# Row halves, a third score bank and a longer lead in a 32-head cross attention

## The reference, cut to what matters

```
n  = layernorm(x)                                  # 4 x 256 x 256
q  = n.reshape(4, 256, 32, 8)                      # 32 heads of 8
k = v = ctx.reshape(4, 256, 8, 8)                  # 8 groups, 4 heads share one
p  = softmax(q @ k.T / sqrt(8))                    # 256 x 256 for each head and batch
x  = x + (p @ v).reshape(4, 256, 256)
```

## Time and profile before

| | |
|---|---|
| median of 3 runs | 805.69 us (805.66 to 806.32) |
| the profiled execution's own time | 806.62 us |
| its span in the trace | 804.8 us |
| PE, DVE, ACT, POOL busy over the span | 89%, 72%, 53%, 25% |
| feed-forward stage | ends at 467 us |
| cross attention | 572.3 to 705.5 us of the span |
| its first and last value product | 599.42 and 702.61 us |

### The profile page before, as it was taken

How to read it: one execution, slowest core, us unless ns; L and a number is a source line. 1 busy time by engine, 2 the same in 40 slices (tenths; PEclk the granted TensorE clock), 3 DMA queues, 4 the chain that set the end, 5 groups by cost and what they waited for, 6 DMA issues and landing times. The chain is left out here.

```text
span 804.8 us, 13314 instructions
## 1 busy us (share of the span) xinstructions
PE 716.4 (89%) x4826; PEld 464.7 (58%) x4826; DVE 577.6 (72%) x1117; ACT 425.7 (53%) x888; POOL 198.6 (25%) x298
## 2 busy tenths in 40 slices
PE   5999989999999999999746569999489999879997
PEld 3555666666676766666422435566344444468886
DVE  5578678686767768677489855575669999665665
ACT  4558754544636454462659555555356666533322
POOL 2423010303113030321317124220121111362450
PEclk9999999999999999999979679999859999969999
DMA  4725432120211112010052016220110323303111
GB/s 121 188 67 159 152 73 69 51 56 25 79 26 56 30 51 75 6 44 14 15 162 49 9 28 176 68 55 2 32 31 22 88 64 88 113 2 107 60 46 53
DMA packets 50272, 52.50 MB, mean 65 GB/s; under 512 B 10116, under 2 KB 40900, under 8 KB 50100
## 3 DMA queue, kind: packets, MB, share of 16 engines
q1 hardware_dynamic: 49574, 51.32, 23.3%
q10 hardware_dynamic: 634, 0.33, 0.2%
HBM read 26.84 MB, written 2.04 MB: 36 GB/s over the span
## 5 line engine op out<-in xcount | busy, mean ns | idle before, releaser
L427 DVE TENSOR_REDUCE a_nm<-ps 128x2 f32<-128x512 f32 (+1 forms) x112 | 75.3, 688 | 28.1 <-PE ps L723 19.4
L2500 DVE TENSOR_REDUCE x_nm<-ps 128x2 f32<-128x512 f32 x128 | 84.9, 686 | 12.4 <-PE ps L2641 10.1
L2585 ACT ACTIVATE x_pt<-ps 128x1024 f32<-128x1024 f32 x64 | 62.5, 1021 | 34.6 <-PE ps L2669 33.9
L1537 PE MATMUL ps<-m_xp,m_mp 128*128 128x512 f32 x288 | 75.4, 398 | 1.0 <-DVE m_wr L1227 1.0
L1408 ACT ACTIVATE m_junk<-ps,m_nm 128x256 bf16<-128x256 f32 x128 | 58.7, 485 | 22.7 <-DVE m_nm L1244 22.7
L1191 POOL TENSOR_SCALAR fw<-fw,finv 128x256 f32<-128x256 f32 x24 | 11.7, 486 | 216.3 <-PE ps L1615 216.3
L2641 PE MATMUL ps<-kx,a_qs 96*128 96x256 bf16 x256 | 53.1, 296 | 8.1 <-DMA a_qs<-a_ks 6.4
L1537 PEld LDWEIGHTS ps<-m_xp,m_mp 128*128 128x128 f32 x288 | 50.8, 188 | 14.7 <-issue 5.3
L3069 PE MATMUL ps<-x_xp,x_wp 128*128 128x512 f32 x216 | 55.2, 406 | 0.0
L1207 DVE TENSOR_TENSOR m_qcs<-ps,mw_tab 64x512 f32<-64x512 f32 x64 | 44.0, 688 | 7.3 <-PE ps L1537 4.2
L1214 DVE TENSOR_TENSOR m_qcs<-ps,mw_tab 128x512 f32<-128x512 f32 x64 | 41.1, 684 | 7.5 <-PE ps L1537 7.2
(11 more groups left out here) (306 smaller groups left out, 1687.3 us busy)
## 6 DMA issues: line engine op xcount, KB each, us to landing
a_qs<-a_parts SPq DMA_DIRECT2D x48, 128.0 KB
a_ks<-a_parts SPq DMA_DIRECT2D x48, 128.0 KB
m_q<-m_qs SPq DMA_DIRECT2D x32, 128.0 KB
x_gb<-scr_g SPq DMA_DIRECT2D x8, 512.0 KB, 3.6
fw<-in_f_w SPq DMA_DIRECT2D x12, 256.0 KB
a_qs<-a_ks SPq DMA_DIRECT2D x48, 64.0 KB
mw_wq<-in_m_wq SPq DMA_DIRECT2D x8, 256.0 KB, 2.9
mw_wo<-in_m_wo SPq DMA_DIRECT2D x8, 256.0 KB, 2.7
```

The source lines that it names most:

```text
L427: dve.tensor_reduce(dst, src, AX.X, ALU.max, negate=True).then_inc(mx_done.sem, 1)
L1537: mm = pe.matmul(c.ps[:, QB_BANKS[k], :], mp[:, p % 2, w, dt, tile * P:(tile + 1) * P], xp[:, x, dt, half_cols(half)], start=((dt, w, x) = ...
L2500: dve.tensor_reduce(nm[:, n % ITEMS, QT * u:QT * u + QT], c.ps[:, u % 2, :].rearrange("p (t k) -> p t k", t=QT), AX.X, ALU.max, negate=Tru ...
L2585: act.activation(pt[:, n % 2, kt, :], c.ps[:, 2 + 2 * kt:4 + 2 * kt, :].rearrange("p b n -> p (b n)"), ACT.Exp, scale=SCALE).then_inc(exp_ ...
```

## The change

- Scores contract 48 rows and turned scores 50. Units of 4 items alternate between rows 0 to 49 and rows 64 to 113 of the query tile (`BASES`); the key tile holds its terms and ones twice, once for each half. No zeros are written. A slot holds two units, so a unit waits for the unit six before it.
- `LAG` is 5 and `TLAG` 4. In the loop the scores of item n + 5 and the turned scores of item n + 1 always lie in different row halves, and `side_by_side` issues them interleaved: one score matmul, one turned-score matmul, one score matmul, four times an item.
- From item 5 on scores take banks 0, 1 and 7 in turn. The turned maxima move from bank 7 to the unused half of bank 6 from item 4 on (`max_bank`).
- Both value products and then the transpose of maxima stand at the end of TensorE's loop.
- `outputs` moves from VectorE to ScalarE, at the end of ScalarE's loop. The two exponentials now stand next to each other, and `max_rows` after them.
- The warm-up has a fifth item of scores, after a `max_transpose(3)`.

```diff
-    GROUPS, S_ROWS, T_ROWS, HD = 8, 96, 98, 8
+    GROUPS, S_ROWS, T_ROWS, HD = 8, 48, 50, 8
+    BASES = (0, 64)
...
     def send(self, sp):
+        for base in self.BASES:
+            sp.dma_start(self.kx[base + self.S_ROWS:base + self.T_ROWS, :, :],
+                         self.ones[0:2, :].unsqueeze(1).broadcast_to([2, self.GROUPS, TOK])).then_inc(self.sent.sem, 16)
         for part, done in enumerate((self.hi_done, self.mid_done, self.lo_done)):
             sp.wait_ge(done.sem, 1)
             for term, p in enumerate((0, 1, 2, 0, 1, 0)):
                 if p == part:
-                    sp.dma_start(self.kx[term:TERMS * self.HD:TERMS, :, :], self.parts[:, part, :]).then_inc(self.sent.sem, 16)
-        sp.dma_start(self.kx[self.S_ROWS:self.T_ROWS, :, :],
-                     self.ones[0:2, :].unsqueeze(1).broadcast_to([2, self.GROUPS, TOK])).then_inc(self.sent.sem, 16)
-        sp.wait_ge(self.sent.sem, 16 * (TERMS + 2))
+                    for base in self.BASES:
+                        sp.dma_start(self.kx[base + term:base + self.S_ROWS:TERMS, :, :], self.parts[:, part, :])\
+                            .then_inc(self.sent.sem, 16)
...
-    LAG, TLAG = 4, 3
+    LAG, TLAG = 5, 4
...
+        def own_rows(n, first, last):
+            base = BASES[n // 4 % 2]
+            return slice(base + first, base + last)
+        def queries(n, first, last, h, count=1):
+            at = n % 4 * 4 + h
+            return qx[own_rows(n, first, last), n // 8 % RINGS, at:at + count, :]
+        def score_bank(n, u):
+            i = 4 * n + u
+            return i % 2 if n < LAG else (0, 1, 7)[(i - 4 * LAG) % 3]
+        def max_bank(n):
+            return c.ps[0:MAXR, 7, 0:SEQ] if n < TLAG else c.ps[0:MAXR, 6, SEQ:2 * SEQ]
...
                         if p == part:
-                            sp.dma_start(qx[term:TERMS * HD:TERMS, k % RINGS, :, :], parts[:, dt, part, seq_cols(b)])\
-                                .then_inc(part_in[k].sem, 16)
+                            sp.dma_start(qx[BASES[k % 2] + term:BASES[k % 2] + S_ROWS:TERMS, k // 2 % RINGS, :, :],
+                                         parts[:, dt, part, seq_cols(b)]).then_inc(part_in[k].sem, 16)
...
                     k, step = divmod(n + 6, 4)
                     if RINGS <= k < UNITS and step < 3:
-                        if step == 0:
-                            sp.wait_ge(st_done.sem, st_done.at(8 * (k - RINGS + 1)))
+                        if step == 0 and k >= 2 * RINGS:
+                            sp.wait_ge(st_done.sem, st_done.at(8 * (k - 2 * RINGS + 1)))
                         send(k, step, (hi_done, mid_done, lo_done)[step])
...
                     for u in range(4):
                         dve.wait_ge(s_done.sem, s_done.at(4 * n + u + 1))
                         dve.tensor_reduce(nm[:, n % ITEMS, QT * u:QT * u + QT],
-                                          c.ps[:, u % 2, :].rearrange("p (t k) -> p t k", t=QT),
+                                          c.ps[:, score_bank(n, u), :].rearrange("p (t k) -> p t k", t=QT),
                                           AX.X, ALU.max, negate=True).then_inc(mx_done.sem, 1)
-                def outputs(n):
-                    b, g = place(n)
-                    dve.wait_ge(av_done.sem, av_done.at(n + 1))
-                    if b >= 2 and g == 0:
-                        dve.wait_ge(dense_out.sem, dense_out.at(64 * (b - 1)))
-                    dve.tensor_scalar(av[:, b % 2, g, :], c.ps[:, 6, 0:SEQ], 1.0, None, ALU.mult)\
-                        .then_inc(out_done.sem, 1)
                 def quotients(s):
                     heads = WIDTH[s] // HD
...
                 maxima(2)
                 remainder(3)
                 maxima(3)
+                maxima(4)
                 for n in range(N - LAG):
                     maxima(n + LAG)
-                    outputs(n)
                 for n in range(N - LAG, N):
-                    for s in LAST_SLOTS[n]:
+                    for s in LAST_SLOTS.get(n, ()):
                         quotients(s)
-                    outputs(n)
                 for s in END_SLOTS:
                     quotients(s)
...
                 def max_rows(n):
                     act.wait_ge(tr_done.sem, tr_done.at(n + 1))
-                    act.activation(mT[:, n % ITEMS, :], c.ps[0:MAXR, 7, 0:SEQ], ACT.Copy).then_inc(mt_done.sem, 1)
+                    act.activation(mT[:, n % ITEMS, :], max_bank(n), ACT.Copy).then_inc(mt_done.sem, 1)
                     if n < TLAG:
                         act.wait_ge(mt_done.sem, mt_done.at(n + 1))
                         act.dma_start(shift_rows(n), mT[:, n % ITEMS, :]).then_inc(m_in[n % ITEMS].sem, 16)
+                def outputs(n):
+                    b, g = place(n)
+                    act.wait_ge(av_done.sem, av_done.at(n + 1))
+                    if b >= 2 and g == 0:
+                        act.wait_ge(dense_out.sem, dense_out.at(64 * (b - 1)))
+                    act.activation(av[:, b % 2, g, :], c.ps[:, 6, 0:SEQ], ACT.Copy).then_inc(out_done.sem, 1)
                 def exponentials(n, kt):
                     if n >= 2:
...
                 exponentials(0, 1)
                 max_rows(2)
                 middle(3)
+                max_rows(3)
                 for n in range(N - 1):
                     exponentials(n + 1, 0)
+                    exponentials(n + 1, 1)
                     if n + TLAG < N:
                         max_rows(n + TLAG)
-                    exponentials(n + 1, 1)
+                    outputs(n)
+                outputs(N - 1)
             @block.tensor
             def _(pe):
...
                                               c.ident[:, :])
                     mm.then_inc(xn_tr.sem, 1)
-                def scores(n, u):
-                    if n >= N:
-                        return
-                    b, g = place(n)
+                def may_score(n, u):
                     if u == 0 and n % 4 == 0:
                         pe.wait_ge(part_in[n // 4].sem, part_in[n // 4].at(16 * TERMS))
-                    if n > 0 or u > 1:
-                        pe.wait_ge(mx_done.sem, mx_done.at(4 * n + u - 1))
-                    for qt in range(QT):
-                        mm = pe.matmul(c.ps[:, u % 2, qt * SEQ:(qt + 1) * SEQ],
-                                       queries(slice(0, S_ROWS), n, u).squeeze(1)[:, qt * P:(qt + 1) * P],
-                                       kx[0:S_ROWS, g, seq_cols(b)], start=True, stop=True)
-                    mm.then_inc(s_done.sem, 1)
+                    i = 4 * n + u
+                    if i == 4 * LAG + 2:
+                        pe.wait_ge(mt_done.sem, mt_done.at(TLAG))
+                    elif i > 4 * LAG + 2:
+                        pe.wait_ge(mx_done.sem, mx_done.at(i - 2))
+                    elif i > 1:
+                        pe.wait_ge(mx_done.sem, mx_done.at(i - 1))
+                def score(n, u, qt):
+                    b, g = place(n)
+                    return pe.matmul(c.ps[:, score_bank(n, u), qt * SEQ:(qt + 1) * SEQ],
+                                     queries(n, 0, S_ROWS, u).squeeze(1)[:, qt * P:(qt + 1) * P],
+                                     kx[own_rows(n, 0, S_ROWS), g, seq_cols(b)], start=True, stop=True)
+                def scores(n, u):
+                    may_score(n, u)
+                    score(n, u, 0)
+                    score(n, u, 1).then_inc(s_done.sem, 1)
                 def max_transpose(n):
                     if n >= N:
...
                     pe.wait_ge(nl_done.sem, nl_done.at(n + 1))
                     both = nms[:, n % ITEMS, :, :].rearrange("p a n -> p (a n)").rearrange("p (r t) -> p t r", t=QT)
                     for qt in range(QT):
-                        mm = pe.matmul(c.ps[0:MAXR, 7, qt * P:(qt + 1) * P], both[:, qt, :], c.identb[:, :],
+                        mm = pe.matmul(max_bank(n)[:, qt * P:(qt + 1) * P], both[:, qt, :], c.identb[:, :],
                                        start=True, stop=True)
                     mm.then_inc(tr_done.sem, 1)
-                def scores_t(n, kt):
-                    if n >= N:
-                        return
-                    b, g = place(n)
+                def may_score_t(n, kt):
                     if kt == 0:
                         pe.wait_ge(m_in[n % ITEMS].sem, m_in[n % ITEMS].at(16 * (n // ITEMS + 1)))
                     if n:
                         pe.wait_ge(exp_done.sem, exp_done.at(2 * n - 1 + kt))
                     elif kt:
                         pe.wait_ge(rest_done.sem, rest_done.at(2))
-                    for h in range(0, 4, 2):
-                        mm = pe.matmul(c.ps[:, 2 + 2 * kt + h // 2, :],
-                                       kx[0:T_ROWS, g, b * SEQ + kt * P:b * SEQ + (kt + 1) * P],
-                                       queries(slice(0, T_ROWS), n, h, 2).rearrange("p h q -> p (h q)"),
-                                       start=True, stop=True)
```

(48 more changed lines are left out.)

10 lines of the change are left out of this document (4 added, 6 removed).

## The result

The changed kernel takes 794.52 us (median of 4 runs, 792.98 to 795.49). The kernel before, measured beside it, takes 806.01 (805.66 to 808.08). The ratio is 0.9855, with a 95% interval of 0.984 to 0.987: 1.4% or 11.5 us faster. Forecast were 797.9 and a range from 795 to 810. The profiled execution took 794.62 with a span of 792.8, where the one before took 806.62 with 804.8: 12.0 us less, where the sum had 7.8.

The account below looks back on a forecast made before the run. TensorE was taken to bound the kernel without a gap, VectorE close behind. Warm-up -5.4, loop +11.5 and last items +1.7 summed to 7.8 us faster: 798.8 from the profiled 806.62, predicted median 797.9, range 795 to 810.

Parts of the forecast that it names:

- What bounded the kernel before: In the loop before, TensorE is the bound without a gap, 3.15 us an item summed; VectorE is close behind.
- the chain: In the loop, from first reduction through fourth score step, products, transposes and next item's first score to its reduction: 2.69 us.
- Halves side by side: In the loop, score and turned-score matmuls in different row halves overlap fully: a block of four takes 0.87 us, not 1.74.
- the item of 2.78: Time of a loop item after the change, ScalarE's sum and 0.05 above VectorE's; ends 2.73 (no stall) and 3.1.
- the loop's term: From item 1's first product to item 28's: 85.96 us before, 74.4 after, a gain of 11.5.
- Warm-up: Before item 1's first product: TensorE stops at max_transpose(3) and the clock rises later, a loss of 5.4 us.
- Hand-over to the last items: At the loop's end: 2.0 us from item 26's first product to item 27's, then 2.9 to item 28's.
- Last items: Items 28 to 31: 2.87 us each instead of 3.42, a gain of 1.7 over three items.
- Key tile: One stage earlier: seven DMAs more on SyncE, the added 4.6 us hidden by 22 us, so no cost.
- Serial halves: Rival for the loop: row halves run one after the other, 3.13 us an item, median 809.5; chance 0.16.
- The longer chain: Rival for the loop: the chain takes 2.9 to 3.0 us and VectorE waits each item, 801 to 805; chance 0.22.
- The low clock: Rival: half clock in the loop, 4.0 us an item; 804 if five items more, 830 if throughout; chance 0.05.

Follow-up runs that it names:

- full-height run: The changed kernel with 96 and 98 rows, zero rows back in the keys, every item in rows 0 to 97: 805.58 us.
- half-maxima run: The changed kernel with each maximum taken over the first 128 of the 256 keys only: 789.31 us.
- split products: The changed kernel with the first value product between the second and third side-by-side steps, so scores come two and two: 801.08 us.

## Why the prediction was right in sign and too small

**What bounded the kernel before.** Right. TensorE waits for nothing in the loop of before, and two form changes fewer on it, in the full-height run, took 0.15 off an item, until the chain stopped it.

**Halves side by side.** Right. Starts coincide (643.77 and 643.77), and a step takes 0.22. (A block of four in 0.87 doesn't stand in the loop, since its fourth step waits.) The run with full rows has 0.44 a step. By the Trainium skill, "TensorE: Matmul & The Clock Gate", section "Measured speedup vs the span model", four row tiles reach 3.07x, which made a step an estimated 0.28; with two halves this trace shows the full factor of 2.

**The failed step: the item of 2.78, "ScalarE's sum and 0.05 above VectorE's".** Both sums add recorded durations as if they were what work costs back to back: 2 x 1.02 + 0.36 + 0.38 on ScalarE, 4 x 0.683 on VectorE, from "three reductions in a row take 2.05 us, so one costs 0.683". The 2.05 of the earlier trace rows hold the last one's full duration, 0.69, and a short wait for scores that didn't split the row: 2.05 - 0.69 is 1.36 for two distances. The right reading is a row in which all scores are there: four in 2.48, less the last one's 0.69, in three distances: 0.60. VectorE's floor is 4 x 0.60 = 2.40 and not 2.73. On ScalarE the prediction called 2.78 an upper bound for back-to-back work and then took it; the half-maxima run shows 2.33. By the Trainium skill, "ScalarE: Activation LUTs", section "What ACT_TABLE_LOAD costs", back-to-back activations overlap by about 93 ns; the trace of the half-maxima run agrees for the copies, 0.36 recorded and 0.26 from start to start, and has a little more for the exponentials, 1.00 to 1.02 and 0.90.

What was left was the chain, which the prediction summed to 2.69 and set aside for the larger sums: the runs show that it alone sets the item, at 2.60. Its links are as written but for the 0.10 between load and matmul, which isn't there: after the wait at 644.95 the matmul starts with its load, some 0.06 after the reduction. Over 25 items 2.78 - 2.64 = 0.14 makes 3.4 us, nearly all of the 3.5 by which the loop's term is off. Two banks instead of three made the item longer by one reduction's 0.60, and shorter reductions made it shorter by as much as each of them: the chain is the bound. That the mean is 2.64 and not 2.60 lies at waits for query rows, 0.9 us on PE in all, and at the first items. Of the signs that the prediction named, reductions stand 0.60 apart and not 0.683, VectorE is idle for 0.11 us in most items instead of never, and the period is 2.60, below 2.73.

**The range.** Its lower end went with 2.73 an item, "no stall", which was not a floor. The chain's own 2.69 would have given 797.9 - 25 x 0.09 = 795.7, and the chain as measured, 2.60, 793.4, which a lower end had to reach. How far the time lies outside is partly chance: 794.52 is 0.5 under 795, and 0.85 us of the gain arose outside the stage. "Under 795" had a chance of 0.04, and for another reason, a hidden warm-up.

**Warm-up.** Right in size, -5.35 for -5.4, and by the mechanism named: TensorE's weight loads stop for 3.04 us at the transposes of item 3, and VectorE idles 2.63 behind it. The clock rose where it was expected, between 607 and 610: 0.50 in 604:608, 0.94 in 608:612. That it agrees to 0.05 is luck in part. The prediction reads that the clock of before is full "some 4 us after TensorE works without gaps". In the trace the last gap ends at 597.62 and the clock is full from about 602.9, and with the same TensorE work it rose near 604.6 in one of the experiments and near 606.8 in another. So these traces give no fixed delay to forecast with.

**Hand-over to the last items.** 1.93 and 2.91 for 2.0 and 2.9.

**Last items.** 2.95 an item for 2.87, gain 1.43 for 1.7. The links that the prediction lists add up to 2.84.

**Key tile.** The stage that sends it was to cost nothing and is 0.41 shorter; the 0.77 ahead of it arise in unchanged code. No run isolates either, and they are smaller than the runs' own spread (792.98 to 795.49).

**The rivals.** Serial halves: excluded. Its price was 809.5 with 3.13 an item; the run where they are serial at full clock has 805.58 with 3.04. The longer chain: excluded here, but two banks and split products show how near it stands, 15.0 and 6.5 us. The low clock: it did not come, but the prediction weighed it for the wrong reason, by TensorE's busy share. The runs with one half are busy for 20.00 of 20 us and stay at 0.50. Had the change filled one half only, the forecast would have missed by over 80 us, so its 0.05 was a hit without the mechanism behind it.

## What to carry to other kernels

Take an engine's cost from the distance of starts in a stretch where nothing is waited for, (length of the row - last duration) / (count - 1), and never from a merged row's length over its count; here the floors built from recorded durations were too high by 0.33 us an item on VectorE and 0.45 on ScalarE. When TensorE is relieved, price the loop as a chain through the scarcest buffer and count how many links of the next engine lie in it: here one bank more or less was 0.60 us an item, all of the gain. A short wait can hide in a row of overlapping matmuls that shows the engine busy without a gap, so compare the row's length with its neighbours'. Before making matmuls narrower, look at the granted clock with the narrow form alone; rows of zeros can be what keeps it up, and a second half in use can replace them.

## What the runs showed of the hardware

- Matmuls over 48 and 50 rows alone left the granted clock at 0.50 through the whole loop (27 x 5.58 = 151 us) without a gap on TensorE in the windows shown (880.96 and 885.75 us, two orders of work). The same matmuls over 96 and 98 rows, the added ones zeros in the keys, had 1.00 (805.58 and 806), and so had two halves of 48 in use (794.52 and 798.99). What in the rows decides it was not measured further.
- Two row halves give the full factor of two: steps of 0.22 against 0.44 us (794.52 and 805.58), starts within 0.01 us of each other, three weight loads a step hidden.
- Overlap of halves arises also where the program issues the matmuls of each half in groups: 798.99 without interleaving by hand, 805.58 without halves. The first turned matmul starts at 654.44, 0.01 behind the first score matmul, with three more ahead of it in the program.
- Starts of equal instructions lie closer than they last: 0.60 for a reduction of 0.683, 0.90 for an exponential of 1.02, 0.26 for a copy of 0.36.
- Two changes fewer between the wide form and the 32-column form in an item gave 0.15 us with the full rows (3.19 to 3.04), while a wait of 0.07 had come in: some 0.1 for each.
- The time at which the clock rises differs between executions with the same TensorE work up to it: near 604.6 in one kernel's trace, near 606.8 in another's (792.24 and 793.74), 0.5 us at the next product.
